# Four graph layers in one kernel: another masked quad in layer 0, another order of the adjacency loads, gate parameters fetched later, the bias added by VectorE

## The reference

```python
support = input @ weight
mask = (adj != 0)
rank = cumsum(mask, axis=1)
deg = rank[:, -1:]
k = minimum(deg, 100.0)
pos = rank - (deg - k)
w = mask * where(pos > 0, 0.5 ** (k - pos), 0.0)
out = w @ support + bias            # layer 0
```

## Time and profile before

| | |
|---|---|
| median of 3 runs | 452.27 us (451.43 to 452.58) |
| the profiled execution | 452.59 us, of which its span 450.6 us |
| TensorE (PE) busy | 422.6 us, 94% of the span |
| VectorE (DVE) busy | 303.2 us, 67% |
| ScalarE (ACT) busy | 207.1 us, 46% |
| GpSimd (POOL) busy | 119.4 us, 27% |
| mean granted TensorE clock | 0.977 |

### The profile page before, as it was taken

One profiled execution on the slowest core, in us unless ns is written; L12 is line 12 of the kernel. 1 busy time (PEld: TensorE's weight loads), 2 busy tenths in 40 slices (PEclk: granted clock), 3 DMA queues, 4 the chain that ended last, 5 costly groups with the idle time before them and its releaser, 6 DMA issues.

```text
span 450.6 us, 6372 instructions
## 1 busy us (share of the span) xinstructions
PE 422.6 (94%) x2294; PEld 203.0 (45%) x2294; DVE 303.2 (67%) x808; ACT 207.1 (46%) x349; POOL 119.4 (27%) x155
## 2 busy tenths in 40 slices
PE   5299799999999999999999999999999999999991
PEld 1034234443444434455555455555444444445471
DVE  3575959775867596556746537768758666567873
ACT  2277567767776687617544434344312212021200
POOL 8112613211510020014211212343333343401111
PEclk9779999999999999999999999999999999999997
DMA  8999999999999992001100110000000010100000
GB/s 115 152 168 108 107 107 108 107 113 111 107 109 112 110 108 37 0 1 23 25 12 13 23 25 1 2 0 1 1 1 12 13 23 14 29 20 25 12 25 23
DMA packets 24894, 23.70 MB, mean 53 GB/s; under 512 B 14368, under 2 KB 16288, under 8 KB 24864
## 3 DMA queue, kind: packets, MB, share of 16 engines
q0 software_dynamic: 9360, 16.78, 37.2%
q1 hardware_dynamic: 15216, 6.33, 5.8%
q10 hardware_dynamic: 288, 0.20, 0.2%
HBM read 69.44 MB, written 1.05 MB: 156 GB/s over the span
## 4 chain that ended last, share of the span: by engine, by line
PE 80%; DVE 9%; DMA 3%; issue 2%; POOL 2%; ACT 2%; POOLq 0%; DVEq 0%
PE Y L924 42%; PE both L837 17%; PE Y L816 8%; PE Y L828 3%; PE both L795 2%; PE both L798 2%; DMA xrow<-in_xrow 2%; PE both L790 2%; PE both L844 2%; DVE work L559 2%; DMA adjT<-in_adjT 1%; POOL rstd L242 1%; PE both L802 1%; ACT wgt L358 1%; DVE work L491 1%
## 5 line engine op out<-in xcount | busy, mean ns | idle before, releaser
L924 PE MATMUL Y<-adjT,S 128*128 128x512 fp8e4 (+1 forms) x1056 | 232.9, 373 | 0.5 <-POOL S L257 0.5
L924 PEld LDWEIGHTS Y<-adjT,S 128*128 128x128 f16 x1056 | 101.6, 98 | 109.8 <-POOL S L257 1.5
L358 ACT ACTIVATE wgt<-both 128x512 int16<-128x512 f32 x192 | 114.0, 597 | 45.5 <-PE both L837 38.1
L242 POOL TENSOR_TENSOR rstd<-stat,mhalf 128x4 f32<-128x4 f32 (+2 forms) x29 | 37.6, 1295 | 175.8 <-DVE stat L464 175.8
L837 PE MATMUL both<-adjT,fix 128*128 128x512 fp8e4 x192 | 74.1, 386 | 1.5 <-DMA adjT<-in_adjT 0.7
L837 PE MATMUL both<-adjT,tri 128*128 128x512 fp8e4 x192 | 74.8, 389 | 0.0
L816 PE MATMUL Y<-wgt,S 128*128 128x512 bf16 x192 | 74.1, 386 | 0.0
L485 DVE SCALAR_TENSOR_TENSOR work<-Y,yT 64x512 f32<-64x512 f32 x30 | 20.8, 694 | 57.2 <-ACT yT L320 56.8
L320 ACT ACTIVATE yT<-Y 64x512 f32<-64x512 f32 x30 | 17.6, 587 | 86.8 <-PE Y L924 59.6
L270 POOL DMA_DIRECT2D adjT<-in_adjT x63 | 33.8, 551 | 66.7 <-DMA adjT<-in_adjT 66.7
L559 DVE SCALAR_TENSOR_TENSOR work<-work,adjT 128x1024 int16<-128x1024 int16 x32 | 42.9, 1361 | 0.0
(11 more groups left out here) (115 smaller groups left out, 385.3 us busy)
## 6 DMA issues: line engine op xcount, KB each, us to landing
adjT<-in_adjT POOLq DMA_DIRECT2D x63, 256.0 KB, 39.7
out_rows<-xrow SPq DMA_DIRECT2D x7, 128.0 KB, 1.9
xrow<-in_xrow SPq DMA_DIRECT2D x1, 640.0 KB, 8.3
hrow<-in_w_gates SPq DMA_DIRECT2D x1, 512.0 KB, 13.4
biases<-in_biases SPq DMA_DIRECT2D x1, 416.0 KB, 7.6
x<-S SPq DMA_TRANSPOSE x24, 2.4
xrow<-in_xrow SPq DMA_DIRECT2D x1, 256.0 KB, 4.6
adjT<-in_adjT POOLq DMA_DIRECT2D x2, 128.0 KB, 6.4
```

What stands on the lines that cost most here:

```text
L242: nc.gpsimd.tensor_tensor(rstd[:, 0:blocks], stat[:, 2, 0:blocks], mhalf[:, 0:blocks], ALU.pow)\
L358: nc.scalar.activation(wgt[:, c, tiles % 2, :], V[c][:, :], ACT.Relu).then_inc(w_ready[c], 1)
L924: mm = nc.tensor.matmul(bank(layer, g)[:, 0:nb * P], S[layer % 2][:, jb, :], cols[:, jb, :], start=(jb == 0), stop=(jb == JB - 1), skip_gr ...
```

## The change

- `MASKED = (5, 2)`: quads 5 and 2 are masked (the third and the sixth in the walk). The slots are 0 to 7 for quads 7 and 6, 8 for quad 5, 9 to 16 for quads 4 and 3, 17 for quad 2, 18 to 25 as before.
- The loads of a quarter come in another order (`ORDER`): the pairs of a masked quad stand between those of other quads. Pairs 11 and 10 (quad 5) are loads 2 and 4 of a quarter, pairs 5 and 4 (quad 2) are loads 8 and 10.
- SP fetches the 64 values of the layer-0 bias by themselves, behind the first part of `xrow`. The other biases and the gate parameters (`gate_pack`, now in the second half of `x16`) are fetched when load 15 has landed. `w_y` stays behind load 3.
- VectorE adds the bias in the first quarter, ahead of its first `sum_quad`. POOL's instruction is gone.
- In quarters 1 to 3 VectorE does the whole of `rows0`, POOL's root included, and the split before it masks the first quad. The sum of the second masked quad stands in the middle of the mask of the first, behind its second set of weights.
- The gate parameters are prepared in quarter 1, behind both masks. Their two small products stand in slot 20 of quarter 1.
- The tables of the masked products and of the filling products are new. Two of the 16 filling products go to slot 0 of the next quarter, or behind the last slot of the last one. In layers 1 to 4 the `combine` calls stand a few products later.

```diff
-MASKED = (6, 2)
+MASKED = (5, 2)
...
-        gate_pack = hrow[:, 0:JB // 2, :].rearrange("p b d -> p (b d)")
+        gate_pack = x16[:, N // 2:N].bitcast(F32)
...
+        ORDER = [15, 14, 11, 13, 10, 12, 9, 8, 5, 7, 4, 6, 3, 2, 1, 0]
+
+        def landing(q, pair):
+
+            return q * JP + ORDER.index(pair)
...
+                if i == 0:
+                    sp.dma_start(bias0, a["biases"][:, 0:D].to_broadcast([P, D])).then_inc(bias0_in, 16)
             sp.wait_ge(load[3], 16)
-            sp.dma_start(biases[:, :], a["biases"].to_broadcast([P, 13 * D])).then_inc(biases_in, 16)
             sp.dma_start(w_y[:, :], a["w_y"]).then_inc(w_y_in, 16)
+            sp.wait_ge(load[NLOAD - 1], 16)
+            sp.dma_start(biases[:, D:13 * D], a["biases"][:, D:13 * D].to_broadcast([P, 12 * D])).then_inc(biases_in, 16)
             sp.dma_start(gate_pack, a["w_gates"]).then_inc(gate_in, 16)
...
-                    jp = JP - 1 - n
+                    jp = ORDER[n]
...
-                    if i == 2 * NLOAD - 2:
-                        pool.wait_ge(const_ready, CONSTS)
-                        pool.wait_ge(biases_in, 16)
-                        pool.wait_ge(s_ready, G)
-                        nc.gpsimd.tensor_tensor(xrow[:, :, :], xrow[:, :, :],
-                                                bias0[:, None, :].to_broadcast([P, JB, D]), ALU.add).then_inc(bias_added, 1)
...
-                i = q * JP + 2 * (G - 1 - quad)
+                i = landing(q, 2 * quad + 1)
...
-                i += 1
+                i = landing(q, 2 * quad)
...
-            def mask_quad(q, quad):
+            def mask_quad(q, quad, between=None):
...
+                if between is not None:
+                    between()
                 pass_tile(1, p0, seen2)
...
+            dve.wait_ge(bias0_in, 16)
+            dve.wait_ge(s_ready, G)
+            nc.vector.tensor_tensor(xrow[:, :, :], xrow[:, :, :], bias0[:, None, :].to_broadcast([P, JB, D]), ALU.add)\
+                .then_inc(bias_added, 1)
             sum_quad(0, MASKED[0])
             mask_quad(0, MASKED[0])
...
+            def gate_weights():
...
             for q in range(Q):
                 if q >= 1:
                     sum_quad(q, MASKED[0])
-                    rows0(q - 1, False)
-                    mask_quad(q, MASKED[0])
-                    rows0_out(q - 1)
+                    rows0(q - 1)
                     split_rows0(q - 1)
-                for quad in MASKED[1:]:
-                    sum_quad(q, quad)
-                    mask_quad(q, quad)
+                    mask_quad(q, MASKED[0], lambda: sum_quad(q, MASKED[1]))
+                if q == 0:
+                    sum_quad(q, MASKED[1])
+                mask_quad(q, MASKED[1])
+                if q == 1:
+                    gate_weights()
...
-            FILL = {17: (0, 1), 18: (2, 3, 4), 19: (5, 6), 20: (7,), 21: (8,), 22: (9, 10), 23: (11, 12), 24: (13, 14), 25: (15,)}
...
+            FILL = {11: (0,), 12: (1,), 13: (2,), 17: (3, 4), 18: (5,), 19: (6, 7), 20: (8,), 21: (9,), 22: (10,), 23: (11,), 24: (12,), 26: (13,), -1: (14, 15)}
+            MASKED_AT = {12: ((5, 3, 0),), 13: ((5, 3, 1),), 14: ((5, 2, 0),), 15: ((5, 2, 1),), 16: ((5, 1, 0), (5, 1, 1),), 17: ((5, 0, 0), (5, 0, 1),), 21: ((2, 3, 0), (2, 3, 1),), 22: ((2, 2, 0), (2, 2, 1),), 23: ((2, 1, 0),), 24: ((2, 1, 1),), 25: ((2, 0, 0), (2, 0, 1),)}
+            MASKED_AT_FIRST = {12: ((5, 3, 0), (5, 3, 1),), 14: ((5, 2, 0), (5, 2, 1), (5, 1, 0), (5, 1, 1),), 16: ((5, 0, 0), (5, 0, 1),), 21: ((2, 3, 0), (2, 3, 1),), 22: ((2, 2, 0), (2, 2, 1),), 23: ((2, 1, 0),), 24: ((2, 1, 1),), 25: ((2, 0, 0), (2, 0, 1),)}
...
-                product(1, 2, 0, 1)
+                product(1, 2, 1, 2)
                 combine(0, 7)
-                product(1, 2, 1, 24)
-                product(1, 3, 0, 7)
+                product(1, 2, 2, 24)
+                product(1, 3, 0, 10)
                 open_gates()
```

More of the change, by code:

```diff
@@ L620, in _ @@
                                     ALU.mult).then_inc(const_ready, 1)
[L621 to L630, removed]
+            def gate_weights():
+                dve.wait_ge(gate_in, 16)
+                did(nc.vector.tensor_scalar(wx16[:, :, 0, :], w_h, GATE / SCALE, None, ALU.mult))
+                after()
+                nc.vector.scalar_tensor_tensor(out=wx16[:, :, 1, :], in0=w_h, scalar=GATE / SCALE, in1=wx16[:, :, 0, :],
+                                               op0=ALU.mult, op1=ALU.subtract).then_inc(gate_const, 1)
+                dve.wait_ge(biases_in, 16)
+                nc.vector.tensor_tensor(gbias[:, :, D:3 * D], gbias[:, :, D:3 * D], brz, ALU.add).then_inc(gate_const, 1)
+                dve.wait_ge(gate_const, 2)
+                nc.vector.tensor_scalar(gbias[:, :, :], gbias[:, :, :], GATE, None, ALU.mult).then_inc(gate_const, 1)
+                dve.wait_ge(gate_prod, 2)
+                prod = gates[0][:, 0:4:2, 0:3 * D]
+                did(nc.vector.tensor_scalar(wm16[:, :, 0, :], prod, GATE, None, ALU.mult))
+                after()
+                nc.vector.scalar_tensor_tensor(out=wm16[:, :, 1, :], in0=prod, scalar=GATE, in1=wm16[:, :, 0, :],
+                                               op0=ALU.mult, op1=ALU.subtract).then_inc(gate_const, 1)
+                dve.wait_ge(gate_const, 4)
             for q in range(Q):
@@ L865, in slot, with fill @@
                     combine(0, 2 * q - 1)
-                for quad, k, c in MASKED_AT.get(s, ()):
-                    weigh_masked(q, quad, k, c)
-                for u in FILL.get(s, ()) if q >= 1 else ():
+                if q == 1 and s == 20:
+                    pe.wait_ge(rows0_ready, 1)
+                    pe.wait_ge(gate_in, 16)
+                    for l in range(2):
+                        mm = nc.tensor.matmul(gates[0][:, 2 * l, 0:3 * D], w_m[0:D, l, :], w_i[0:D, l, :], start=True, stop=True)
+                        mm.then_inc(gate_prod, 1)
+                for quad, k, c in (MASKED_AT if q else MASKED_AT_FIRST).get(s, ()):
+                    weigh_masked(q, quad, k, c)
+                fill(q, s)
+            def fill(q, s):
+                units = FILL.get(s, ()) if q >= 1 else ()
+                if q == Q - 1 and s == NS:
+                    units += FILL[-1]
+                if q >= 2 and s == 0:
+                    q, units = q - 1, FILL[-1]
+                for u in units:
                     jb = (q - 1) * 2 * B + u // 2
@@ L880, in layer0 @@
                         elif kind == "tile" and at % 2 == 1:
-                            i = q * JP + (JB - 1 - at) // 2
+                            i = landing(q, at // 2)
                             pe.wait_ge(load[i % NLOAD], 16 * (i // NLOAD + 1))
@@ L968, in layer1 @@
-                product(1, 5, 0, 15)
+                product(1, 4, 21, 32)
+                product(1, 5, 0, 17)
                 combine(1, 4)
-                product(1, 5, 15, 32)
-                product(1, 6, 0, 15)
+                product(1, 5, 17, 32)
+                product(1, 6, 0, 17)
                 combine(1, 5)
-                product(1, 6, 15, 32)
-                product(1, 7, 0, 15)
+                product(1, 6, 17, 32)
+                product(1, 7, 0, 17)
                 combine(1, 6)
-                product(1, 7, 15, 32)
+                product(1, 7, 17, 32)
@@ L997, in layer2 @@
+                product(2, 4, 0, 17)
                 combine(2, 3)
-                product(2, 4, 15, 32)
-                product(2, 5, 0, 15)
+                product(2, 4, 17, 32)
+                product(2, 5, 0, 17)
                 combine(2, 4)
-                product(2, 5, 15, 32)
-                product(2, 6, 0, 15)
+                product(2, 5, 17, 32)
+                product(2, 6, 0, 17)
                 combine(2, 5)
-                product(2, 6, 15, 32)
-                product(2, 7, 0, 15)
+                product(2, 6, 17, 32)
@@ L1066, in layer4 @@
-                product(4, 6, 0, 21)
+                product(4, 5, 27, 32)
+                product(4, 6, 0, 22)
                 combine(4, 5)
-                product(4, 6, 21, 32)
+                product(4, 6, 22, 32)
                 product(4, 7, 0, 8)
```

117 lines of the change are left out of this document (52 added, 65 removed).

## The result

The changed kernel takes 445.45 us (median of 4 runs, 445.42 to 445.51), against 452.38 us before (4 runs). The ratio is 0.9857, 95% interval 0.9839 to 0.9875: faster. The medians lie 6.9 us apart; the ratio, which comes from all the runs, says 1.4%. The forecast was 446.8 us, in a range of 444.0 to 449.8. The profiled execution took 445.43 us, of which its span 443.2 us (mean granted clock 0.984).

What follows compares the result with a forecast made beforehand. Time was taken as TensorE's work plus its gaps, which loads can make until the adjacency is in. P(3) 187.5 + 257.6 behind it = 445.1 span, 5.5 under 450.6; 452.3 - 5.5 = 446.8 us, range 444.0 to 449.8.

Steps and rivals of the forecast that it cites:

- gap two: TensorE's 2.88 us wait at slot 20 of quarter 0, released by VectorE's weights of quad 2, slowed during POOL's bias add.
- the price of the bias add and of the root: Layer 0: bias add on VectorE taken as 2.4 us, POOL's root as 1.64 us rather than 2.61.
- the period of quarters 2 and 3: Layer 0: each of these quarters was forecast to take 43.2 us instead of 43.5.
- half microsecond of margin at slot 16: Quarters 2 and 3: k=1 weights ready at P + 26.2, slot 16 ends at P + 26.7, so no stall.
- the rivals with a wait at slot 16: Three quarters: stalls of 0.5 to 1 us, 448.3 to 449.8 (14%); or with lowered clock, 453.5 or more (7%).
- the signs that were named: First gap ends near 18.1 with a load; no slot 20 gap; VectorE idles about 1.7 us before the root multiply.
- The shifted `combine` calls of layers 1 to 4 I cost at nothing: Layers 1 to 4: moving these calls costs or gains nothing; the stretch was forecast at 257.6 us against 257.4.
- P(3): Moment VectorE starts to pick the degrees of quarter 3: forecast 187.5 us, against 193.2 before.
- P(0): Moment VectorE starts to pick the degrees of quarter 0: forecast 55.3 us against 62.4, 7.1 ahead.
- what remains of gap one: Quarter 0: rest of the 7.1 us gain, from TensorE's 7.83 us wait at slot 4 for VectorE's sum of quad 6.
- Quarter 1 gives part back: Quarter 1: moved 928 KB fall behind load 15, load 20 stays at 62.9, `rows0` 2.1 us late; lead falls to 5.1.
- P(1): Moment VectorE starts to pick the degrees of quarter 1: forecast 101.1 us, against 106.2 before.

Runs made afterwards that it cites:

- e3: The kernel before, with the bias added by VectorE behind its first mask and nothing else changed: 447.85 us, ratio 0.9902.
- e7: The changed kernel with the bias added by POOL ahead of load 31, as before the change: 448.61 us, ratio 0.9927.
- e6: The changed kernel with the loads in the old order (pair 15 down to 0) in all quarters: 447.92 us, ratio 0.9911.
- e1: The changed kernel with the old places of the combine calls in layers 1 to 4: 448.40 us, ratio 0.9913.
- e2: The kernel before with only the new places of the combine calls in layers 1 to 4: 449.52 us, ratio 0.9943.
- e8: The changed kernel with the 64 bias values fetched behind the third part of xrow instead of the first: 444.83 us, ratio 0.9841.
- e9: e8 with the other biases and the gate parameters fetched behind load 21 instead of load 15: 444.69 us, ratio 0.9839.
- e12: e8 with the other biases and the gate parameters fetched behind load 27: 443.77 us, ratio 0.9822.
- e4: The kernel before with the bias on VectorE behind the first mask and the new combine places of layers 1 to 4: 445.58 us, ratio 0.9849.
- e5: The changed kernel with the other biases and the gate parameters fetched behind load 3 again: 447.29 us, ratio 0.9896.

## Why the prediction was right, and where it wasn't

**Right, by row.** Which two gaps there are and who releases them; that POOL's bias add is the cause of gap two (e3, e7); the price of the bias add and of the root; the period of quarters 2 and 3, 43.17 against a forecast 43.2; VectorE's chain in them to 0.2 us, with its half microsecond of margin at slot 16; that the rivals with a wait at slot 16 fail in the changed kernel. That wait exists: e6 shows it as soon as the chain begins 2.5 us later. Of the signs that were named, the first gap did end with a load (at 18.68), slot 20 has no gap, and VectorE waits 1.78 us before the multiply by the root.

**The step that failed: "The shifted `combine` calls of layers 1 to 4 I cost at nothing: the stretch has too few gaps to win or lose half a microsecond".** They are worth 2.8 to 3.0 us (e1, e2), over 40% of the gain, and the prediction's own sign of being wrong, a change by more than 0.5 us behind P(3), came. The busy sum hid them. Matmul ends are modelled, so a delayed start of 0.1 us inside a run of matmuls leaves no idle time of TensorE. The view of waits of the weight loads had 9.2 us in 22 short idles in the kernel before, put down to no engine, and the forecast didn't use it.

**A term mis-sized: P(0).** Forecast 55.3, measured 58.2. Of the 2.9 us, 1.15 are slot 15's start (39.45 instead of 38.3: load 11 came 3.1 us behind load 10, and the early fetch of the bias delayed the first loads by some tenths, e8), and 1.7 are the lower clock behind that wait, which the forecast had priced behind gap two and not here. The early fetch it had at nothing: it put 928 KB behind load 15, but it is 896 (384 and 512), and the other 32 KB go ahead of the loads. The 7.1 us that it gave to P(0) also held 2.0 for "what remains of gap one". No run shows them: e3 keeps gap one and has P(0) at 57.3.

**Quarter 1 gives part back.** The forecast had it and it is so, but it named two loads. Load 20 only delays VectorE, which matters if P(0) is early enough; load 27, in slot 15, is the one that binds (e9 against e12). In the changed kernel itself TensorE waited for neither, since P(0) was late. VectorE waited 1.43 us for load 20, but its statistics began at P(0) + 8.0 all the same. P(1) is P(0) + 44.1, the plain period with the gate products. The forecast's 101.1 is 0.8 more than its own terms: 83.5, the nine slots, 17 products and the gate products make 100.3.

**The parts and their worth.** Bias on VectorE: 4.5 us alone (e3), 3.2 in the new order (e7), by medians. Combine places: 2.8 to 3.0. The rest together: about nothing (e4 against the change), because the loads bound quarter 0 under both orders; the later parameters are worth 1.8 (e5) and the new order 2.5 (e6) only once quad 5 is the masked one.

**What stays open.** Why the clock fell behind slot 15's wait in the changed kernel (1.98 us), e1 (2.06) and e5 (2.25), and not in e8 (1.92), e12 (1.74), e9 (2.19) and e7 (2.31): the length of the wait doesn't sort them. That it falls in some executions and not in others would explain the two groups of e5, 1.7 us apart, which is its price. The spreads of e7 (2.4 us) and e12 (1.6) have no two such groups. Only one execution of each was profiled, and the mean clock of the others doesn't tell the groups apart (0.984 in a run of e5 of 448.14 us and in one of 446.42), so this is argued, not shown.

## What to carry to other kernels

- A stretch in which the bound engine looks busy can still hold a per cent. Compare the start of each small operation with the end of the run of work ahead of it (count times pace), and look at the weight loads' idles, before a shift of such an operation is costed at nothing.
- A gap at the start of a stretch that is fed by loads is not always worth its length. What counted here is when the last load that is waited for lands; the loads pile up during the gap and the engine then runs through them.
- Parameters belong behind the last load that anyone waits for, if they are still in time for their first use, and that load is found by moving them (e9, e12), not from the first wait that one sees.

## What was not expected of the hardware

- A fetch of 64 values to 128 partitions ahead of the other parts of `xrow` went with a start of TensorE at 8.5 us and not at 6.9 (the change against e8). The other traces agree: 8.5 to 8.7 in all five kernels with the early fetch, 6.7 to 7.3 in the nine without it. Its 32 KB are an eighth of what a load writes, and those are 2.46 us apart; why it costs 1.6 us isn't shown.
- The landings are 2.46 us apart as a rule, but load 11 often takes longer: 3.1 us behind load 10 in the changed kernel and in e8, 3.4 in e4, 3.9 in e2, and 2.9 or more in eleven of the fourteen traces. It isn't the order of the loads: e2 and e4 share the old one with the kernel before and e3, where it was 2.4. In e2 and e4 the load behind it then came after 2.0 and 1.7 us, so a part of the delay was made up.
- The granted clock behind equal waits can differ: 0.56 in the changed kernel and 1.00 in e8 over 3.85 us, behind waits of 1.98 and 1.92 us.
